# Routed experts with 8 weight sets: hidden layer computed transposed, tokens fetched two tiles ahead, loops written out

## The reference, cut to what matters

```python
x = x + _L0_xattn_ref(_layernorm(x), ctx_512, ...)
x = x + _L0_ffn_ref(_layernorm(x), Wr, br, W1, b1, W2, b2)   # 8 experts, one per token
x = x + _L1_xattn_ref(_layernorm(x), ctx_512, ...)
x = x + _L1_ffn_ref(_layernorm(x), router_w, w1, w2)         # 64 experts, four per token

def _L0_ffn_ref(x, Wr, br, W1, b1, W2, b2):     # W1 8x512x128, W2 8x128x512
    expert_idx = jnp.argmax(xf @ Wr.T + br, axis=-1)
    h = jax.nn.relu(jnp.einsum('td,efd->etf', xf, W1) + b1[:, None, :])
    y = jnp.einsum('etf,edf->etd', h, W2) + b2[:, None, :]
    out = y[expert_idx, jnp.arange(xf.shape[0])]
```

## Time and profile before

| | before |
|---|---|
| time, median of 3 runs | 2928.42 us (2924.88 to 2937.17) |
| profiled execution: own time / span | 2937.18 / 2935.4 us |
| busy in the whole span: PE, DVE, ACT, POOL | 2548.0, 2051.4, 1581.9, 1590.4 us |
| experts of layer 0 (635 to 900 us): PE, DVE, ACT, POOL busy | 189.28, 98.64, 40.56, 140.66 of 265 us |
| the same, granted clock | 0.91 |
| experts of layer 1 and final stage (2700 to 2935 us): PE, POOL busy | 143.25, 122.55 of 235 us |
| the same, granted clock | 0.50 |

### The profile page before, as it was taken

How to read it: one execution, slowest core, us unless ns; L and a number is a source line. 1 busy time by engine, 2 the same in 40 slices (tenths; PEclk the granted TensorE clock), 3 DMA queues, 4 the chain that set the end, 5 groups by cost and what they waited for, 6 DMA issues and landing times. The chain is left out here.

```text
span 2935.4 us, 102242 instructions
## 1 busy us (share of the span) xinstructions
PE 2548.0 (87%) x34936; PEld 1878.4 (64%) x34937; DVE 2051.4 (70%) x6396; ACT 1581.9 (54%) x3466; POOL 1590.4 (54%) x2644
## 2 busy tenths in 40 slices
PE   6899999967774899999999999999999999845566
PEld 4666666645553677777777777777777777633333
DVE  3677777763332578888888888888888888643345
ACT  3445555531111577777777777777777777621122
POOL 1222222225553456666666666666676666546544
PEclk9899999989998899999999999999999999855555
DMA  8211111111112000000000000000000000001137
GB/s 235 64 36 36 36 35 33 35 25 37 35 36 104 5 8 6 5 4 5 5 5 5 5 5 5 5 5 5 5 5 5 5 5 5 6 16 38 38 102 204
DMA packets 152447, 92.68 MB, mean 32 GB/s; under 512 B 42111, under 2 KB 144145, under 8 KB 151714
## 3 DMA queue, kind: packets, MB, share of 16 engines
q1 hardware_dynamic: 133410, 74.58, 8.8%
q0 software_dynamic: 18944, 16.91, 2.2%
HBM read 53.63 MB, written 39.03 MB: 32 GB/s over the span
## 5 line engine op out<-in xcount | busy, mean ns | idle before, releaser
L1148 POOL TENSOR_SCALAR st_h<-st_h 128x1 f32<-128x1 f32 x192 | 36.6, 191 | 564.3 <-DVE st_h L1352 562.8
L1240 POOL DMA_INDIRECT list_d<-pay,dest x256 | 269.8, 1054 | 130.6 <-issue 93.8
L1651 DVE TENSOR_REDUCE rdx<-core 128x16 f32<-128x1920 f32 (+1 forms) x128 | 284.4, 2222 | 39.5 <-PE core L782 38.4
L1072 ACT ACTIVATE kbd<-core 128x1024 f32<-128x1024 f32 (+1 forms) x256 | 247.0, 1016 | 44.1 <-PE core L820 40.2
L820 PE MATMUL core<-rdx,cst 32*128 32x128 f32 (+1 forms) x4096 | 241.1, 277 | 10.4 <-issue 9.5
L815 PE MATMUL core<-qT,pTm 32*128 32x128 f32 (+1 forms) x4096 | 238.1, 285 | 0.6 <-ACT rdx L1058 0.4
L820 PEld LDWEIGHTS core<-rdx,cst 32*128 32x128 f32 (+1 forms) x4096 | 193.9, 185 | 19.8 <-issue 19.7
L782 PEld LDWEIGHTS core<-pTm,qT 32*128 32x128 f32 x4096 | 125.8, 186 | 99.1 <-issue 93.7
L815 PEld LDWEIGHTS core<-qT,pTm 32*128 32x128 f32 (+1 forms) x4096 | 175.2, 184 | 19.3 <-issue 10.9
L1029 ACT ACTIVATE pT<-bank 128x512 f32<-128x512 f32 x72 | 43.0, 597 | 228.8 <-PE bank L723 130.8
L1089 ACT ACT_TABLE_LOAD x128 | 164.2, 1283 | 2.3
(11 more groups left out here) (242 smaller groups left out, 7509.0 us busy)
## 6 DMA issues: line engine op xcount, KB each, us to landing
c_d<-zeros SPq DMA_DIRECT2D x64, 256.0 KB
xn_d<-xnS SPq DMA_DIRECT2D x128, 64.0 KB
vS<-c_d SPq DMA_DIRECT2D x32, 256.0 KB, 3.3
oT<-c_d SPq DMA_DIRECT2D x32, 256.0 KB, 3.4
big<-in_w SPq DMA_DIRECT2D x1, 4096.0 KB, 12.3
yb<-y_d SPq DMA_DIRECT2D x64, 64.0 KB, 1.8
list_d<-pay,dest POOLq DMA_INDIRECT x256
out<-kT SPq DMA_DIRECT2D x64, 64.0 KB, 2.7
```

Source lines behind the costliest of these rows:

```text
L1072: af(pTb[0:u.T, 2 * k:2 * k + 2, :], core[0:u.T, 2 * k:2 * k + 2, :], ACT.Exp, scale=SCALE).then_inc(s_pexp, 1)
L1240: g_.indirect_dma_start(out=list1_d, out_offset=bass.IndirectOffsetOnAxis(ap=dest[:, v.bs, k:k + 1], axis=0), in_=pay[:, v.bs, k, :], in_o ...
L1651: v_.tensor_reduce(nm[:, :].rearrange("p (g k) -> p g k", g=NG)[:, :, 0:4], core[:, :, 0:4 * T].rearrange("p g (c t) -> p g c t", c=4), AX ...
```

## The change

1. The inner product of a layer-0 tile is computed transposed: four matmuls (L730) in which a 128x128 piece of the inner weights is stationary and the tokens move, so that the result is 512 x tokens. The four transpositions `hidden_t0` and their places in PE's order are gone.
2. The weights of the tile's expert are first copied by ACT (`weights0`, L1017) into one of two buffers `w1S` (in the unused tile kbd), under a new semaphore `s_wS`; ACT reads the expert from the table for it.
3. The bias is added per partition (`b1T0`, one column per 128 hidden values), and its load shrinks from a 2048 KB broadcast to 16 KB. ACT's relu reads SBUF in place of PSUM.
4. The transposition of tokens in PE's turn u is that of tile u+2 in place of u+1; so is DVE's copy. POOL's order and `LAG` stay.
5. `ring_rounds` and the loops over `step_c` are written out in full on all engines: 72, 64 and 64 turns.
6. Two thresholds of layer 1's waits on `s_htr` are counted without layer 0, which no longer raises it.

The diff, without the hunks that repeat (the loops over `step_c` of ACT, POOL, DVE and SP, and the declaration of `s_wS`):

```diff
@@ -76,7 +76,7 @@
...
         w2T0 = big[:, 4096:8192].rearrange("p (e c d) -> p e c d", e=E0, c=4)
-        b1bc0 = big[:, 8192:12288].rearrange("p (e f) -> p e f", e=E0)
+        b1T0 = big[:, 8192:8192 + 4 * E0].rearrange("p (e c) -> p e c", e=E0)
         w1_1 = big[:, 0:8192].rearrange("p (e f) -> p e f", e=E1)
@@ -202,6 +202,7 @@
...
         pTb = kbd
+        w1S = kbd[:, 0:2, :]
         pTmb = (prob, pT)
@@ -390,17 +392,9 @@
-            rounds = n // RING
-            for i in range(2):
-                for k in range(RING):
-                    step(i, k, True)
-            if rounds > 3:
-                with eng.Fori(2, rounds - 1) as i:
-                    for k in range(RING):
-                        step(i, k, True)
-            for k in range(RING):
-                step(rounds - 1, k, k < RING - 1)
-            after(rounds - 1)
+            for j in range(n):
+                step(j // RING, j % RING, j < n - 1)
+            after(n // RING - 1)
         def earlier(i, k, d):
@@ -461,7 +455,7 @@
...
                 sp.dma_start(w2T0, t["w2T0"]).then_inc(s_ffnw, 16)
-                sp.dma_start(b1bc0, t["b10"].partition_broadcast(P)).then_inc(s_ffnw, 16)
+                sp.dma_start(b1T0, t["b10"]).then_inc(s_ffnw, 16)
                 sp.dma_start(b2bc0, t["b20"].partition_broadcast(P)).then_inc(s_ffnw, 16)
@@ -715,14 +709,6 @@
...
                                       max_val=E0 - 1)
-            def hidden_t0(u, q):
-                pe.wait_ge(s_h, u.count(1, 1))
-                if positive(n := u.count(1, -1)):
-                    pe.wait_ge(s_hT, n)
-                for c in range(4):
-                    last = tr(bank[4 + q][:, c * P:(c + 1) * P], h0[:, q, c * P:(c + 1) * P], ident)
-                last.then_inc(s_htr, 1)
-
             def out0(u, q, e):
@@ -736,27 +722,25 @@
...
                 q = k % 2
-                e = expert(pe, i, k)
                 pe.wait_ge(s_gT, u.count(1, 1))
...
                     pe.wait_ge(s_h, n)
-                mm(bank[2 + q][:, :], xgT[:, q, :],
-                   w1T0[:, bass.ds(e, 1), :].rearrange("p o f -> p (o f)"),
-                   start=True, stop=True).then_inc(s_hps, 1)
+                pe.wait_ge(s_wS, u.count(1, 1))
+                for c in range(4):
+                    last = mm(bank[2 + q][:, c * P:(c + 1) * P], w1S[:, q, c * P:(c + 1) * P],
+                              xgT[:, q, :], start=True, stop=True)
+                last.then_inc(s_hps, 1)
                 if earlier(i, k, 2):
                     out0(u.shift(-2), q, expert(pe, i, k - 2))
-                if earlier(i, k, 1):
-                    hidden_t0(u.shift(-1), 1 - q)
-                if more:
-                    tokens_in(u.shift(1), 1 - q)
+                if i * RING + k + 2 < TILES0:
+                    tokens_in(u.shift(2), q)
             def end0(last):
-                u = Unit(0, last, RING, RING - 1)
-                out0(u.shift(-1), 0, expert(pe, last, RING - 2))
-                hidden_t0(u, 1)
-                out0(u, 1, expert(pe, last, RING - 1))
-
-            tokens_in(Unit(0, 0, RING, 0), 0)
+                for k in (RING - 2, RING - 1):
+                    out0(Unit(0, last, RING, k), k % 2, expert(pe, last, k))
+
+            for k in range(2):
+                tokens_in(Unit(0, 0, RING, k), k)
             ring_rounds(pe, TILES0, tile0, end0)
@@ -964,11 +948,8 @@
...
                     .then_inc(s_ov, 1)
-            for k in range(RC):
-                step_c(0, k)
-            with pe.Fori(1, NB // RC) as i:
-                for k in range(RC):
-                    step_c(i, k)
+            for j in range(NB):
+                step_c(j // RC, j % RC)
@@ -1023,13 +1004,29 @@
             def relu(u, q):
-                act.wait_ge(s_htr, u.count(1, 1))
+                act.wait_ge(s_h, u.count(1, 1))
                 if positive(n := u.count(1, -1)):
                     act.wait_ge(s_yps, n)
-                af(h0T[:, q, :], bank[4 + q][:, :], ACT.Relu).then_inc(s_hT, 1)
-
-            ring_rounds(act, TILES0, lambda i, k, more: relu(Unit(0, i, RING, k), k % 2),
-                        lambda last: None)
+                af(h0T[:, q, :], h0[:, q, :], ACT.Relu).then_inc(s_hT, 1)
+
+            def weights0(j):
+
+                e = act.value_load(etile_i[0:1, bass.ds(j, 1)], min_val=0, max_val=E0 - 1)
+                if positive(j - 1):
+                    act.wait_ge(s_hps, j - 1)
+                af(w1S[:, j % 2, :], w1T0[:, bass.ds(e, 1), :].rearrange("p o f -> p (o f)"), ACT.Copy)\
+                    .then_inc(s_wS, 1)
+
+            def tile0(i, k, more):
+                relu(Unit(0, i, RING, k), k % 2)
+                if i * RING + k + 2 < TILES0:
+                    weights0(i * RING + k + 2)
+
+            act.wait_ge(s_map, 1)
+            act.wait_ge(s_ffnw, 64)
+            weights0(0)
+            weights0(1)
+            ring_rounds(act, TILES0, tile0, lambda last: None)
             def inputs_b(h):
@@ -1515,10 +1506,11 @@
...
                 if positive(n := u.count(1, -1)):
-                    dve.wait_ge(s_htr, n)
-                v_.tensor_tensor(h0[:, q, :], bank[2 + q][:, :],
-                                 b1bc0[:, bass.ds(e, 1), :].rearrange("p o f -> p (o f)"), ALU.add)\
-                    .then_inc(s_h, 1)
+                    dve.wait_ge(s_hT, n)
+                v_.tensor_tensor(h0[:, q, :].rearrange("p (c t) -> p c t", c=4),
+                                 bank[2 + q][:, :].rearrange("p (c t) -> p c t", c=4),
+                                 b1T0[:, bass.ds(e, 1), :].rearrange("p o c -> p (o c)")
+                                 .unsqueeze(2).to_broadcast([P, 4, P]), ALU.add).then_inc(s_h, 1)
             def result0(u, k, e):
@@ -1534,15 +1526,16 @@
...
                     result0(u.shift(-2), (k - 2) % RING, expert(i, k - 2))
-                if more:
-                    tokens_T(u.shift(1), 1 - k % 2)
+                if i * RING + k + 2 < TILES0:
+                    tokens_T(u.shift(2), k % 2)
             def end0(last):
...
                     result0(Unit(0, last, RING, k), k, expert(last, k))
-            tokens_T(Unit(0, 0, RING, 0), 0)
+            for k in range(2):
+                tokens_T(Unit(0, 0, RING, k), k)
             ring_rounds(dve, TILES0, tile0, end0)
@@ -1730,12 +1723,13 @@
...
                 dve.wait_ge(s_sil, Unit(0, u.i, RING, u.r).count(1, 1))
-                dve.wait_ge(s_htr, u.count(1, -1))
+                if positive(n := Unit(0, u.i, RING, u.r).count(1, -1)):
+                    dve.wait_ge(s_htr, n)
                 v_.tensor_tensor(glu[:, q, q * I1:(q + 1) * I1], bank[2 + q][:, I1:2 * I1], silu[:, q, 0:I1],
...
             def gate_T(u, q):
-                dve.wait_ge(s_htr, u.count(1, 1))
+                dve.wait_ge(s_htr, Unit(0, u.i, RING, u.r).count(1, 1))
                 dve.wait_ge(s_yps, u.count(1, -1))
@@ -1841,7 +1832,7 @@
...
     o["w2T0"] = c(a["L0_ffn_W2"].reshape(E0, P, 4, P).transpose(3, 0, 2, 1))
-    o["b10"] = a["L0_ffn_b1"]
+    o["b10"] = c(a["L0_ffn_b1"].reshape(E0, 4, P).transpose(2, 0, 1))
     o["b20"] = a["L0_ffn_b2"]
```

More of the change, by code:

```diff
@@ L286, in build_program @@
         s_map = sem("s_map")
+        s_wS = sem("s_wS")
         s_ids = [sem(f"s_ids{k}") for k in range(RING)]
@@ L561, in _ @@
                 load_c(0, k)
-            with sp.Fori(0, NB // RC - 1) as i:
+            for i in range(NB // RC - 1):
                 for k in range(RC):
@@ L1131, in step_c @@
                 af(poT[0:E1, k, :], bank[k % 2][0:E1, 0:P], ACT.Copy).then_inc(s_poT, 1)
-            for k in range(RC):
-                step_c(0, k)
-            with act.Fori(1, NB // RC) as i:
-                for k in range(RC):
-                    step_c(i, k)
+            for j in range(NB):
+                step_c(j // RC, j % RC)
         @block.gpsimd
@@ L1326, in step_c @@
                                  ALU.add).then_inc(s_cs, 1)
-            for k in range(RC):
-                step_c(0, k)
-            with pool.Fori(1, NB // RC) as i:
-                for k in range(RC):
-                    step_c(i, k)
+            for j in range(NB):
+                step_c(j // RC, j % RC)
         @block.vector
@@ L1790, in step_c @@
                     .then_inc(s_fin, 1)
-            for k in range(RC):
-                step_c(0, k)
-            with dve.Fori(1, NB // RC) as i:
-                for k in range(RC):
-                    step_c(i, k)
+            for j in range(NB):
+                step_c(j // RC, j % RC)
 CST_WIDTH = 238 + 80 + 512 + 128
```

## The result

The changed kernel takes 2974.09 us (median of 4 runs, 2971.0 to 2977.21), the kernel before 2930.56 (4 runs beside it): the ratio is 1.0148, 95% interval 1.0132 to 1.0165. The profiled execution took 2974.68 us with a span of 2972.9. By stage of the two profiled executions, the difference of the spans, +37.5 us, is made up so: the first gather of layer 0 comes 4.9 us earlier (652.34 against 657.22), the experts of layer 0 from the first gather to the last scatter take 305.9 in place of 259.2 us (+46.7), attention of layer 1 +9.1, layer 1's experts -9.4 from the first tile's matmul to the last one's, the final stage -3.9; what is left is between the last two. (The medians are 43.5 us apart: the profiled run of before was its slowest.)

What follows compares the result with a forecast made beforehand. No engine is full; a chain within the layer-0 tile sets the pace. Ring +25.6, stop +5, ends -6, clock +22 and bias load -4.9 sum to +42 on the profiled 2937.2; against the median 2928.4 that gives 2970, range 2925 to 2998.

Steps and rivals of the forecast that it cites:

- the loop through GpSimd: Layer-0 experts: gather waits behind an earlier tile's scatter; loop spans two turns, not three, 7.73 us, and sets the pace.
- a ring shorter than summed: Rival, layer-0 experts: loop takes 6.9 to 7.2 us, 3.5 per tile, total 2920 to 2938; chance 0.12.
- the one in which it doesn't bind: Rival, layer-0 experts: loop under 6.7 us, work and jitter give 2.9 to 3.05 per tile, total 2885; chance 0.08.
- the one in which the clock stays high: Rival, layer-0 experts: ring binds but the clock's 22 us fall away, +20, total 2948; chance 0.18.
- writing out removes stops: Rival: layer 1's stops come from the loop's branch; some 35 us would go, total 2913 to 2935; chance 0.10.
- Two of my signs: PE waits for layer-0 gathers more than 60 times; over 5 us change outside layer-0 experts and first 90 us means wrong.
- The ring's size: Layer-0 tiles 5 to 71: 3.87 us per tile, 255.4 against 229.8, so +25.6 (+13 to +36).
- my low case: Layer-0 ring with 2.22 and 0.11 for first and last link: 7.36 us for two turns, 3.68 per tile.
- The clock: Layer-0 experts: PE's repeated gather waits lower the clock; 0.4 of tiles at 1.2 GHz, 0.83 us each, +22 (0 to +45).
- The stop: Layer-0 experts: a stop like the earlier trace's, with PE idle for 4.9 us, will come again, +5.
- The ends and the bias load: First five and last two layer-0 turns and tail, -6; 2.1 MB less bias load before attention, -4.9.
- Outside: Written-out loops in layer 1's experts and final stage: no gain, +-3 us.

Runs made afterwards that it cites:

- lag five: Changed kernel with GpSimd scattering layer-0 tile v-5 instead of v-4 behind the gather of tile v; 2922.86 us, ratio 0.9976 to the kernel before.
- the filled gaps: Changed kernel with six more identity transpositions per layer-0 tile on PE, ahead of the tokens' transposition; 2950.13 us, ratio 1.0034 to the kernel before.

## Why the prediction was right, and where its sizes were off

Predicted 2970, measured 2974; slower by 1.5%. The mechanism was right; that the number is so near is luck, as the terms below show. The main step, that the loop through GpSimd spans two turns and binds, is shown from four sides: the links add up in the changed kernel's rows, a lag of five takes 51 us off its stage, and in the kernel before both a lag of three and a lookahead of two, each alone, bring the same wait and 2.3 and 2.7%. The rival of a ring shorter than summed, the one in which it doesn't bind and the one in which the clock stays high did not come true. That writing out removes stops came true in a small part, see below.

Two of my signs did not come out as written. I expected more than 60 waits for the gather and had 44: with a loop over two turns, PE waits about once per pair, which my own sum already said. And a change of more than 5 us outside the experts of layer 0 was to mean that I was wrong: attention of layer 1 took 9.1 us more and layer 1's experts 9.4 less. The two cancel, which is luck too.

*The ring's size.* Forecast 3.87 per tile. The sum of the links measured at full clock is 3.68, my low case; the average over the eight full-clock distances is 3.81. I took 2.43 from inner matmul to result; it is 2.12, and 0.17 in place of 0.27 at the end of the loop. The other three links were right to 0.04 us. The term is +13 us by the links and +21 by the average, not +25.6. The Trainium skill's figure (DMA: Bandwidth & Descriptors, section "Anatomy of one DMA — SWDGE (gpsimd) path"), worked out as an estimate to 2.15 us for the gather, is below the 2.57 seen here.

*The clock.* Forecast +22. What is left above the ring is 66 x (4.24 - 3.68) = +37 by the links, or 66 x (4.24 - 3.81) = +28 by the average; it holds the clock and all else, such as five gathers of over 3.0 us. The share of low clock was right (0.81 over the stage is 38% of the time at 1.2 GHz), its price was not: the pair with one slow product takes 8.71, that is 1.35 more than 7.36, and over all distances of two turns those with low clock in them take 8.61 against 7.61. I took 0.83 for each slow tile and 0.4 of the tiles, 0.66 for a pair. That the clock is a part of it is shown by the filled gaps, which gave back 66 x 0.22 = 15 us. The Trainium skill (TensorE: Matmul & The Clock Gate, section "HAM oscillation — how this bites in real kernels") describes waits for transfers between bursts of matmuls, after which PE runs throttled anew each time. The rows at 843.40 and 852.21 agree in kind, and so does with a transposition within the gap; the wait that ends at 827.76 did not bring the fall.

*The stop.* I added 5 us for a stop like that of the earlier trace rows; there was none. The ring slows GpSimd down, to one gather per 4.24 us and rows of at most four transfers behind the start, where lag five has one per 3.53 us and 18 rows of six. Up to here it is 50 (13 + 37, or 21 + 28 with rounding) against 25.6 + 5 + 22 = 53: a ring too large, a clock too cheap and an addend that wasn't there cancel.

*The ends and the bias load.* First gather to tile 5 19.9 in place of 21.3, and tile 71 to last scatter 5.8 in place of 8.1: -3.7, not -6. The first gather comes 4.9 us earlier, as forecast; that this is the 2 MB was not tried by itself, but the nine traces with the small load have it at 652.1 to 653.8 and the five with the large one at 653.9 to 660.4, on average 4.3 later.

*Outside.* I forecast 0 +- 3 for the written-out loops. Layer 1's experts gained 9.4 and attention before them lost 9.1. The first is real, since all ten written-out kernels take 194.6 to 198.2 us there and the four with loops 200.1 to 203.9: layer 1 stops every four tiles in loops and every five or so written out. The second cannot be the edit of the experts, and over all kernels attention took 1702 to 1721 us; four with the loops had 1702 to 1708, ten written-out ones 1707 to 1721. Whether that is chance stays open.

*What I had wrong about the gain that could be had.* My rival on the faster side had 2.9 to 3.05 us per tile and 2885 once the ring is gone. With the ring gone it is 3.53. By PE's and GpSimd's busy times the gain was there; the price of GpSimd's transfers at their full pace was not in my sum: no stops are seen at 3.21 us per pair, and at 2.94 they are there. Layer 1's average of 3.3 with stops hinted at it.

## What to carry to other kernels

When a load is used a turn earlier, count over how many turns the loop from its use back to its issue now spans; an in-order queue that issues it behind another wait ties it to a result, and one turn fewer can turn hidden latency into the pace. Change the lag of that queue together with the lookahead. And when an engine issues transfers back to back, compare the average with its stops, not the best distance: a slower, even pace can be the faster one, as in layer 0 here, or cost the same, as in layer 1.

## What the runs showed that was not expected

**Stops behind GpSimd's transfers.** At 2.6 to 2.9 us per pair of 64 KB indirect transfers, VectorE and ScalarE get PE's completions some 3 us late, in lag five only 1.1 to 1.3 us after a burst has ended; at 3.21 us per pair no wait of this kind is left in the stage, with GpSimd just as busy. A useless operation of 0.74 us in each pair of layer 0 took about 0.7% off the lag-five kernel (0.9903 with it, 0.9976 without; 0.9891 with it in both layers). What holds the completions is not settled: a backlog behind the transfers fits all paces tried, but no run shows the thing itself, and none slows GpSimd without giving it work.

**Useless work on PE** made the changed kernel faster too, 1.0034 against 1.0148, with the granted clock raised from 0.81 to 0.94 over 656 to 938 us.
